# Reading x in five transfers behind the last scatters, the weights among the late sums, and moving the middle region's end from tile 256 to 272

## What is computed

```
edge_index = jnp.stack([src, dst])                    # dst is sorted
h = relu(layernorm(x)); x = x + L0(h, edge_index, edge_attr)   # sums of edge_attr by src and by dst, MLP
h = relu(layernorm(x)); x = x + L1(h, edge_index, edge_attr)   # sum of edge_attr by dst, MLP
h = relu(layernorm(x)); x = x + L2(h, edge_index)              # two graph convolutions
h = relu(layernorm(x)); x = x + L3(h, edge_index, edge_attr)   # message MLP, mean by dst, update MLP
```

## Time and profile before

| | us |
|---|---|
| median of 3 runs | 1222.26 |
| lowest, highest | 1221.35, 1224.45 |
| the profiled execution | 1228.04 |
| its span | 1226.1 |
| place_and_count and what is ahead of it | 0 to 566.2 |
| TensorE's warm-up and VectorE's first sum of sum_blocks | 566.2 to 570.4 |
| late sums, first matmul to last | 570.4 to 621.1 |
| ends of sum_blocks | 621.1 to 624.8 |
| layers | 624.8 to 1226.1 |

### The profile page before, as it was taken

How to read it: one execution, slowest core, us unless ns; L and a number is a source line. 1 busy time by engine, 2 the same in 40 slices (tenths; PEclk the granted TensorE clock), 3 DMA queues, 4 the chain that set the end, 5 groups by cost and what they waited for, 6 DMA issues and landing times. The chain is left out here.

```text
span 1226.1 us, 31788 instructions
## 1 busy us (share of the span) xinstructions
PE 1103.4 (90%) x9479; PEld 935.1 (76%) x9480; DVE 892.4 (73%) x3127; ACT 627.4 (51%) x1792; POOL 698.2 (57%) x712
## 2 busy tenths in 40 slices
PE   6999797999999989934888899989799999999997
PEld 3666454888887878833865799974799999999985
DVE  6999776678777889895768854456467777777763
ACT  7665544888988789775733311024223333333322
POOL 4777777777777777782000000006767777777771
PEclk9999897899999999977988899987999999999998
DMA  7675334655565666544871000017868888888841
GB/s 238 190 202 156 106 106 118 163 156 158 156 160 150 183 197 185 168 134 137 242 39 55 2 2 2 1 46 214 241 185 234 222 220 232 242 220 231 230 141 45
DMA packets 176362, 187.16 MB, mean 153 GB/s; under 512 B 43828, under 2 KB 136353, under 8 KB 176057
## 3 DMA queue, kind: packets, MB, share of 16 engines
q1 hardware_dynamic: 141858, 136.10, 41.7%
q0 software_dynamic: 22400, 46.35, 12.4%
q10 hardware_dynamic: 11928, 2.62, 1.1%
HBM read 138.78 MB, written 44.28 MB: 149 GB/s over the span
## 5 line engine op out<-in xcount | busy, mean ns | idle before, releaser
L2610 POOL DMA_INDIRECT between<-p_table,src_g x284 | 279.2, 983 | 362.2 <-DMA p_table<-n_nm 271.9
L981 POOL DMA_INDIRECT rows_by_block<-h_t,mean_bc x312 | 313.0, 1003 | 106.4 <-issue 85.9
L471 PE MATMUL acc<-ones_b 128*128 128x128 bf16 (+1 forms) x925 | 159.8, 298 | 47.2 <-PEq L911 33.2
L1112 DVE TENSOR_TENSOR between<-between,acc 128x600 f32 x208 | 161.5, 776 | 49.3 <-PE acc L1266 39.1
L1255 PE MATMUL acc<-n_nm 128*128 128x384 bf16 (+1 forms) x832 | 144.8, 298 | 32.1 <-issue 20.8
L2751 ACT ACTIVATE between<-acc 128x128 f32<-128x128 f32 x138 | 38.3, 278 | 223.4 <-PE acc L2868 197.5
L1076 DVE TENSOR_SCALAR n_nm<-iota_w,agg_sum 128x600 bf16<-128x600 f16 x416 | 144.3, 388 | 0.0
L1000 ACT ACTIVATE away<-iota_b,agg_sum 128x128 bf16<-128x128 bf16 x416 | 140.9, 385 | 0.0
L1255 PEld LDWEIGHTS acc<-n_nm 128*128 128x128 bf16 x832 | 73.4, 99 | 80.4 <-issue 30.3
L471 PEld LDWEIGHTS acc<-ones_b 128*128 128x128 bf16 x925 | 72.6, 100 | 74.5 <-issue 58.6
L2851 PE MATMUL acc<-weights,between 128*128 128x128 f32 x568 | 124.9, 302 | 0.0
(11 more groups left out here) (296 smaller groups left out, 2555.7 us busy)
## 6 DMA issues: line engine op xcount, KB each, us to landing
h_t<-in_edge_rows SPq DMA_DIRECT2D x78, 260.0 KB, 3.6
between<-in_edge_columns SPq DMA_DIRECT2D x35, 512.0 KB
between<-in_dst SPq DMA_DIRECT2D x35, 288.0 KB
held<-rows_by_block SPq DMA_DIRECT2D x69, 130.0 KB
h_t<-rows_by_block SPq DMA_DIRECT2D x34, 260.0 KB, 3.5
by_dst<-q_whole_table SPq DMA_DIRECT2D x138, 64.0 KB
x_nm<-rows_by_block SPq DMA_DIRECT2D x30, 260.0 KB
agg_sum<-in_edge_rows SPq DMA_DIRECT2D x26, 260.0 KB
```

The lines of the kernel that those rows point to most:

```text
L471: pe.matmul(acc[:, bank * BANK + skip:(bank + 1) * BANK].rearrange("p (a n) -> p a n", n=P), ones_b[:, :], ones_b[:, :].rearrange("p (a n) ...
L981: pool.indirect_dma_start(rows_by_block, bass.IndirectOffsetOnAxis(ap=place_in_table[:, t:t + 1], axis=0), row_group(g)[:, j, :], None).th ...
L1112: dve.tensor_tensor(between[:, :, bass.ds(first, W)], between[:, :, bass.ds(first, W)], acc[:, o:o + NB * WS].rearrange("p (b w) -> p b w" ...
L2610: pool.indirect_dma_start(got[:, q, j * D:(j + 1) * D], None, p_table, bass.IndirectOffsetOnAxis(ap=src_g[:, n * G + j:n * G + j + 1], axi ...
```

## The change

Three things are changed.

1. **x in pieces.** Instead of one transfer of 24 blocks behind the last early sum there are five of 5, 5, 5, 5 and 4 blocks. Piece k waits until all scatters of group 98+k have landed. The 53 rows of the last block follow the fifth piece. `X_LOADS` counts the six.
2. **The weights later.** `load_rest` is divided in four parts of 4, 6, 5 and 6 transfers. SyncE issues them inside `sum_blocks`, behind the late reads 9, 12, 15 and 18. What waited for all 23 transfers waits for x's six; SyncE at the end of `sum_blocks` and TensorE ahead of its work behind read 44 wait for the 21.
3. **Regions.** The middle region takes tiles 132 to 271, with the same 155 slots (seven of them in blocks 8 to 15 instead of 7 to 14); the late one has 155 slots instead of 181 (6 a block up to block 15, then 7, the last 3). The middle region's reads stand two pairs later, at pairs 150 to 199. The bounds of the check on filled slots follow.

```diff
-TILES_MID = 256
+TILES_MID = 272
...
 def cap_mid(b):
-    return 7 if 7 <= b < 15 else 6 if b < NB - 1 else 3
+    return 7 if 8 <= b < 16 else 6 if b < NB - 1 else 3
...
 def cap1(b):
-    return 7 if b < 15 else 8 if b < NB - 1 else 4
+    return 6 if b < 16 else 7 if b < NB - 1 else 3
...
+        X_LOADS, REST_LOADS = 6, 21
+
-        def load_rest(sp):
+        def load_rest(sp, part):
...
+            if part == 0:
+                for to, of in ((w_l0, l0[0]), (w_l1, l1[0]), (w_msg, l3[0]), (w_upd, l3[4])):
+                    load(to[:, :, :], of.rearrange("(k p) f -> p k f", p=P))
+            if part == 1:
+                load(w2_msg[:, :], l3[2])
+                for k, of in enumerate((l0[1], l1[1], l2[1], l3[5], l3[3])):
+                    load(b_cols[0:of.shape[0], k:k + 1], of.rearrange("(p a) -> p a", a=1))
+            if part == 2:
+                for to, of in ((w2_l0, l0[2]), (w2_l1, l1[2]), (w1_g, l2[0]), (w2_g, l2[2]), (w2_upd, l3[6])):
+                    load(to[:, :], of)
+            if part == 3:
+                for k, of in enumerate((l0[3], l1[3], l2[3], l3[7], l3[1])):
+                    load(b_rows[:, k, :], of.partition_broadcast(P))
+                load(b1_row[:, :], l2[1].partition_broadcast(P))
...
-            read_pairs = {(78 + r * 68 // wide_reads if r < wide_reads else 148 + (r - wide_reads) * 52 // NB): r for r in range(len(early_reads))}
+            read_pairs = {(78 + r * 68 // wide_reads if r < wide_reads else 150 + (r - wide_reads) * 52 // NB): r for r in range(len(early_reads))}
...
-                    sp.dma_start(x_nm[:, 0:NB - 1, :], x[0:(NB - 1) * P, :].rearrange("(b p) f -> p b f", p=P)).then_inc(loaded.h, 16)
+                    for k in range(X_LOADS - 1):
+                        g = GROUPS - X_LOADS + k
+                        sp.wait_ge(scattered[g % ROWG].h, scattered[g % ROWG].at(SC * (g // ROWG + 1)))
+                        b0, b1 = 5 * k, min(5 * k + 5, NB - 1)
+                        sp.dma_start(x_nm[:, b0:b1, :], x[b0 * P:b1 * P, :].rearrange("(b p) f -> p b f", p=P)).then_inc(loaded.h, 16)
                     sp.dma_start(x_nm[0:NLAST, NB - 1, :], x[(NB - 1) * P:N, :]).then_inc(loaded.h, 16)
-                    load_rest(sp)
-                    sp.wait_ge(loaded.h, loaded.at(16 * 23))
+                    sp.wait_ge(loaded.h, loaded.at(16 * X_LOADS))
...
-                    dve.wait_ge(loaded.h, loaded.at(16 * 23))
+                    dve.wait_ge(loaded.h, loaded.at(16 * X_LOADS))
...
+                        if r >= 2 * LB_IN - 3 and r % 3 == 0 and r // 3 - 3 < 4:
+                            load_rest(sp, r // 3 - 3)
...
+                    sp.wait_ge(loaded.h, loaded.at(16 * REST_LOADS))
...
                             pe.wait_ge(late.h, late.at(4))
+                            pe.wait_ge(loaded.h, loaded.at(16 * REST_LOADS))
```

More of the change, by code:

```diff
@@ L80 @@
 TILES_HERE = base2(NSB)
-TILES_MID = 256
+TILES_MID = 272
 GROUPS_MID = TILES_MID // KC
 def cap_mid(b):
-    return 7 if 7 <= b < 15 else 6 if b < NB - 1 else 3
+    return 7 if 8 <= b < 16 else 6 if b < NB - 1 else 3
 def base_mid(b):
-    return TILES_HERE + 6 * b + min(max(b - 7, 0), 8)
+    return TILES_HERE + 6 * b + min(max(b - 8, 0), 8)
 LATE_AT = base_mid(NB - 1) + cap_mid(NB - 1)
 def cap1(b):
-    return 7 if b < 15 else 8 if b < NB - 1 else 4
+    return 6 if b < 16 else 7 if b < NB - 1 else 3
 def base1(b):
-    return LATE_AT + 7 * b + max(b - 15, 0)
+    return LATE_AT + 6 * b + max(b - 16, 0)
 SURE2 = (9, 8)
@@ L937, in _ @@
                         if g == ROWG + 3:
-                            zero_ends(base_mid(0), 7, cap_mid(0), TAIL_LATE)
-                            zero_ends(base_mid(7), 8, cap_mid(7), TAIL_MID)
+                            zero_ends(base_mid(0), 8, cap_mid(0), TAIL_LATE)
+                            zero_ends(base_mid(8), 8, cap_mid(8), TAIL_MID)
                         if g == ROWG + 6:
-                            zero_ends(base_mid(15), 9, cap_mid(15), TAIL_LATE)
+                            zero_ends(base_mid(16), 8, cap_mid(16), TAIL_LATE)
                             zero_ends(base_mid(NB - 1), 1, cap_mid(NB - 1), TAIL_LATE)
                         if g == ROWG + 9:
-                            zero_ends(base1(0), 15, cap1(0), TAIL_LATE)
+                            zero_ends(base1(0), 16, cap1(0), TAIL_LATE)
                         if g == ROWG + 12:
-                            zero_ends(base1(15), 9, cap1(15), TAIL_LATE)
+                            zero_ends(base1(16), 8, cap1(16), TAIL_LATE)
                             zero_ends(base1(NB - 1), 1, cap1(NB - 1), TAIL_LATE)
@@ L1168, in _ @@
                             dve.tensor_scalar(upper1[:, NB - 1:NB], base_rows[:, 2, NB - 1:NB], float(cap1(NB - 1) * P), None, ALU.add)
[L1169 to L1171 removed]
+                            dve.tensor_scalar(lower_mid[:, 0:8], base_rows[:, 1, 1:9], -float(TAIL_LATE * P), None, ALU.add)
+                            dve.tensor_scalar(lower_mid[:, 8:16], base_rows[:, 1, 9:17], -float(TAIL_MID * P), None, ALU.add)
+                            dve.tensor_scalar(lower_mid[:, 16:NB - 1], base_rows[:, 1, 17:NB], -float(TAIL_LATE * P), None, ALU.add)
                             dve.tensor_scalar(lower_mid[:, NB - 1:NB], base_rows[:, 1, NB - 1:NB], float((cap_mid(NB - 1) - TAIL_LATE) * P), None, ALU.add)
@@ L1286, in place_and_count @@
             checked.passed(CHECKED_AT_END)
-            loaded.passed(16 * 23)
+            loaded.passed(16 * X_LOADS)
             vec.passed(2 + NB - CHECKED_BY_ACT + 3)
@@ L1596, in sum_blocks @@
             vec.passed(4)
+            loaded.passed(16 * REST_LOADS)
             rooted.passed(2)
```

15 lines of the change are left out of this document (3 added, 12 removed).

## The result

The change makes the kernel slower. Twelve runs of it have a median of 1228.62 us (1224.93 to 1237.1), twelve of before beside them 1222.61 us (1215.56 to 1226.55): a ratio of 1.006, 95% interval 1.0037 to 1.0082, or 7.3 us (4.5 to 10.0); the medians alone are 6.0 us apart. 1225.3 us had been forecast, +3.1, with a time within 0.3% of before as the likeliest case (0.55). The time lies inside the range that was stated (up to 1229.0), but it is a slowdown beyond what the measurement can miss, which had been given 0.33.

A forecast was written before the change was run, and what follows sets the result against it. Bounds: GpSimd's scatters close the count stage; a closed ring of reads sets the late sums, TensorE nearly. Terms 1.6 - 1.5 + 3.0 = +3.1 us on the median of 1222.26; written 1225.3 us, 8-in-10 range 1219.5 to 1229.0.

The forecast's parts named there:

- Part 1: End of the count stage: x read in pieces arrives later, costing +1.6 us (+0.4 to +3.4).
- The door: End of the count stage, when all engines are let on to the late sums: forecast at 567.8 instead of 566.2.
- The stall: GpSimd scatter at 535.28 took 7.56 us instead of 0.96; laid to VectorE's check of counts, so it stays, gain 0.
- Part 2: Late sums: 26 slots fewer save 1.5 us (ends 0 and -4.5).
- Part 3: Late sums: 21 weight issues in four bursts ahead of reads cost +3.0 us (1.0 to 5.5).
- The price of a blocked SyncE: Late sums: when SyncE was held 3.5 us by count and keys issues, some 2 to 2.5 us came through.
- the traffic is over: Count stage, 535 to 543 us: DMA share of 0.23 read as x and weight reads finished, so not causing the long scatter.
- the ring's reads: Late sums as a closed ring: each read goes out when the sum six reads back is done, landing 3.4 us later.
- Rival (c): Late sums: bursts drain the ring of reads, costing 5.5, and x lands late; +7.9 in all, 1230.2 us; chance 0.12.
- a busy TensorE of some 39 us: Sign of a right forecast: TensorE's busy time in the late sums, against 45.5 of 50.7 us before.
- gaps of 1 to 3 us: Sign of a right forecast: gaps before VectorE's hots near reads 13 to 22 of the late sums, with TensorE idle.
- TensorE's new wait behind read 44: Late sums: TensorE's added wait at read 44 is long met by then.

## Why the prediction was right and wrong

**Part 1, right in its mechanism, 0.7 us too high.** The door went from 5.91 to 6.81 behind the last scatter, +0.9 (+1.0 alone) against +1.6, inside 0.4 to 3.4. The last of x went out 2.25 us before the last scatter started, where 1.5 to 1.9 had been counted, and was there 3.74 us after the start of its issue (3.6 from issue to landing had been taken, the issue itself not counted in). For the 53 rows the prediction had named the Trainium skill, "DMA: Bandwidth & Descriptors", "Why a DMA increments its semaphore by 16 and not by 1": by its rule such a transfer goes to one DMA engine. No trace shows a late landing by it: x came as the ordinary reads do. The stall was kept, and stayed in every kernel that kept the check and its pace, with x and the weights ahead of it or not. It is gone with the check alone left out.

The Trainium skill, "SBUF — State Buffer", "SBUF: two separate sides", says that a VectorE operation with two SBUF inputs can hold the port that VectorE and GpSimd share, for the whole of the instruction, against a GpSimd operation that reads SBUF. The trace agrees in kind: the operations of the check take two inputs from SBUF, and the scatter reads its places from SBUF. It differs in extent: back to back they held one scatter for 7.6 us, many operations long. Which access of the scatter is held was not tried.

**Part 2, right alone, larger in company.** Alone it saved 1.5 us of the late sums, as forecast. From the kernel with x in pieces to the same with the regions (both with early weights) it saved 4.5 us, the far end of the range. Each is a difference of single executions with a spread of some 0.5 us, so the 3 us between them are more than spread. TensorE's clock may be most of them: alone, the regions had it at 0.50 for some 3 us and TensorE busy 41.7 us, where the same sums took 40.5 in the other pair; and x in pieces with the old regions began its sums at half clock and was busy 46.5 us, where before was 45.4. That is 1.2 + 1.1 = 2.3 us of the 3, as an upper bound; what is left stays open.

**Part 3, the step that failed: 3.0 us (1.0 to 5.5) forecast, 8.4 and 9.5 measured.** The step was: "The price of a blocked SyncE is in the trace ... of 3.5 us held, some 2 to 2.5 came through", applied burst by burst as 0, 1.0, 1.0 and 2.0, less 1.0 regained. It priced the issue of the 21 transfers, at durations that were right (the bursts took 2.0, 3.1, 2.5 and 2.8 us against 2.2, 3.3, 2.8 and 3.3), and nothing for their service. Three things were left out.

- The bytes. The text itself had the DMA share at 0.75 and 212 GB/s in this stage, and landings as VectorE's largest wait. 1248 KB more through the same engines is an estimated 6.0 us by that row, and 6.05 came out with the long hole removed and the clock at 1.00. That it is the bytes, and not the issues with them, is the better fit and not shown. In place_and_count the same bytes delay nobody: the scatters kept their pace beside a DMA share of 1.02.
- The one source row. It was in the trace of before: the stretch from 535 to 543 us, right behind the last issues of the bias rows, has a share of 0.23 and 55 GB/s. The prediction read this as "the traffic is over". In the change the scatters stand still in the same way, but no bias rows are under way, and the DMA engines move nothing at all:

```profile
536.00:538.00 2.00, 0.00 (x0) 0.00 (x0) 2.00 (x3) 1.97 (x3) 2.00 (x1) 0.50 0.00 0
538.00:540.00 2.00, 0.00 (x0) 0.00 (x0) 1.97 (x3) 2.00 (x1) 2.00 (x1) 0.50 0.00 0
```

So the 55 GB/s of before were for the most part the bias rows (352 KB of some 440), being served slowly. How slowly a kernel shows in which VectorE arrives first: without its check it waited for them until 542.93, 6.8 us after the last of the six was issued at 536.17.

```profile
536.17 0.43 SPq L644 DMA_DIRECT2D b_row<-in_L_gnn_b  x1
...
542.93 4.93 DVE L1191 BATCH_NORM_STATS2 stats<-x_nm 128x6 f32<-128x128 f32 x25 [10.98 <-DMA b_row<-in_L_gnn_b]
```

In before VectorE came at 545.00, after them, and no wait was left to read. With the regions alone it waited for them too, until 546.80, 5.6 us after the last issue:

```profile
546.80 4.93 DVE L1213 BATCH_NORM_STATS2 stats<-x_nm 128x6 f32<-128x128 f32 x25 [3.13 <-DMA b_row<-in_L_gnn_b]
```

Moved in front of the ring's reads the slowness costs 3.4 us: a read lands after 7.25 us, TensorE idles 5.3 us, and its clock is halved for the work that follows.

- The clock. The prediction held it at 1.00 without a word. In the change TensorE was busy 3.5 us longer than with early weights for the same sums, and three of the other kernels with late weights lost as much.

Rival (c) named the right place ("two bursts in a row find no buffer filled ahead, reads 15 to 24") and had the end of 5.5 us, still 3 to 4 too low, since it too was made of issue time. That the sum came out only 3 us too low is an accident of the signs: +0.9 - 4.1 + 9.5 = +6.3 by the stages, where 1.6 - 1.5 + 3.0 had been written. The late sums of 52.1 us that the terms give (50.6 - 1.5 + 3.0) were missed by 4 us, "a busy TensorE of some 39 us" by 5 (44.06, of it some 3 us for 50 matmuls at half clock); "gaps of 1 to 3 us" were there at 578.33 (2.20) and 585.98 (1.54), and the one of 5.74 at 594.77 was not foreseen. TensorE's new wait behind read 44 cost nothing, as said. The chance of 0.12 for (c) was too small above all because no case held a cost of service.

## What to carry to other kernels

A transfer that is moved costs three things: its issue on the queue, its bytes in the traffic of the stage it is moved to, and its service in front of what waits behind it; divide its bytes by the GB/s that the new stage already needs before counting slots on the issuing engine (the estimate fitted here, and was not tested by itself). Look at the granted clock of every stretch before dividing a difference among causes. Ask of each moved transfer how fast it was served where it stood, and don't take a low GB/s behind its issue for a free queue. Long two-input VectorE operations beside GpSimd's indirect DMAs are worth issuing with a gap between them, since the gap is where the other gets in.

## What the runs showed of the hardware

- Transfers that read one DRAM row into 128 partitions, five of 512 bytes and one of 256 behind each other: 69 to 72 GB/s over 4 us with reads queued behind, against 114 and 225 in the same place when the five read 128 different rows. In place_and_count, with VectorE waiting for them, the last of them landed 6.8 and 5.6 us after the last issue began (two executions). Whether it is the one address or something else in the descriptors of such a transfer wasn't tried.
- VectorE's seven two-input operations on 800 words, back to back, held one scatter for 7.6 us, many operations long, not one. With a gap of some 0.04 us between operations one scatter took 2.45 us and the four behind it 1.75 each, one at every second gap.
- 1248 KB more in a stage with a DMA share of 0.71 to 0.75 cost 6.05 us with the clock at 1.00 in both kernels (issues and one one-row transfer of 32 KB are in it), the estimate from the GB/s of before being 6.0. Nine matrices of 832 KB cost 4.75, with the clock at 0.93.
- TensorE, idle for 5.3 us, lost its clock while it idled (1.00 until 594, restart at 595.25) and then ran at 0.50 until some 601.4. A long idle time isn't needed: with the nine matrices it fell near 595 behind waits of 0.9 and 1.1 us, while one of 2.1 us with distinct rows left it at 1.00. Which work of TensorE before the fall decides this was not tested.
